# A fused attention and mixture-of-experts kernel: the value product moved ahead of two max products, and side work spread over the slots

## The reference

```
x = x + layernorm(attention(layernorm(x)))
    # attention: own layernorm, qkv product, 16 heads of 16 dims,
    # softmax(q k^T / 4) v over 1024 keys, projection, plus the residual
x = x + layernorm(ffn(layernorm(x)))
    # ffn: silu(x w1) * (x w2), layernorm over 128, product w3;
    # 512 tokens of batch 0 are routed besides to the best of 8 experts
    # and to a weighted mix of the shared and the expert result
```

## Time and profile before

| | |
|---|---|
| times of three runs | 983.48, 983.86 and 985.3 us, median 983.86 us |
| the profiled execution's own time | 983.9 us |
| its span | 982.1 us |
| busy share of the span | PE 90%, VectorE 81%, ScalarE 68%, GpSimd 32% |
| mean granted clock of TensorE | 0.968 of full speed |

### The profile page before, as it was taken

The page is one execution under the profiler, slowest core; times in us unless marked ns, Lnnn a source line. Parts: engine busy times, 40 slices in busy tenths (PEclk is TensorE's granted clock), DMA queues, the critical chain, the costliest instruction groups (busy, mean ns, idle before and its releaser), DMA issues. The chain is left out here.

```text
span 982.1 us, 14337 instructions
## 1 busy us (share of the span) xinstructions
PE 882.3 (90%) x5188; PEld 319.8 (33%) x5188; DVE 792.7 (81%) x1568; ACT 663.7 (68%) x728; POOL 314.5 (32%) x450
## 2 busy tenths in 40 slices
PE   6879999999999999999999999999989989757985
PEld 3312322222243233322332242322322313136863
DVE  4598879898979878899888879889799788265765
ACT  5128778787877787878877868788677768901110
POOL 4041010005424414139443423255243232822113
PEclk9769999999999999999999999999999989988998
DMA  5631010310320203101411022004310001240001
GB/s 143 105 45 39 16 53 16 73 41 10 90 61 13 93 12 70 38 13 55 89 61 56 12 39 59 23 7 105 91 56 14 11 13 31 85 172 23 1 1 64
DMA packets 52375, 49.08 MB, mean 50 GB/s; under 512 B 17504, under 2 KB 43696, under 8 KB 51920
## 3 DMA queue, kind: packets, MB, share of 16 engines
q1 hardware_dynamic: 51680, 46.91, 19.4%
q0 software_dynamic: 384, 1.05, 0.3%
q10 hardware_dynamic: 240, 0.20, 0.2%
HBM read 18.06 MB, written 9.17 MB: 28 GB/s over the span
## 5 line engine op out<-in xcount | busy, mean ns | idle before, releaser
L1331 DVE TENSOR_REDUCE mx<-ring 128x1 f32<-128x512 f32 x1024 | 633.9, 680 | 110.3 <-PE ring L1038 109.6
L873 ACT ACTIVATE prob<-sc,unscale 128x1024 f32<-128x1024 f32 x512 | 539.1, 1113 | 85.2 <-PE sc L1056 83.9
L1038 PE MATMUL ring<-kp,qp 48*128 48x512 f16 x1024 | 299.4, 395 | 43.5 <-DVE mx L1331 22.5
L1070 PE MATMUL obank<-prob,vaug 128*32 128x512 f32 x2048 | 276.1, 612 | 0.7 <-ACT prob L873 0.6
L1038 PEld LDWEIGHTS ring<-kp,qp 48*128 48x128 f16 x1024 | 74.1, 93 | 361.4 <-DVE mx L1331 301.3
L1056 PE MATMUL sc<-qp,kp 64*128 64x512 f16 x1024 | 167.9, 381 | 14.0 <-ACT prob L873 13.3
L644 POOL TENSOR_TENSOR parts<-qkf,parts 128x1024 f16<-128x1024 f32 x14 | 29.9, 2134 | 209.6 <-ACT parts L803 209.6
L1056 PEld LDWEIGHTS sc<-qp,kp 64*128 64x128 f16 x1024 | 50.4, 95 | 92.3 <-ACT prob L873 83.9
L631 POOL TENSOR_TENSOR hid<-hid,b 128x512 f32<-128x512 f32 x24 | 30.2, 1270 | 110.9 <-ACT hid L827 110.9
L639 POOL TENSOR_TENSOR yA<-yA,sums 128x512 f32<-128x512 f32 x15 | 19.0, 1269 | 131.1 <-DMA sums<-reciprocal_scratch 131.1
L1070 PEld LDWEIGHTS obank<-prob,vaug 128*32 128x32 f32 x2048 | 40.5, 108 | 61.5 <-issue 58.4
(11 more groups left out here) (221 smaller groups left out, 749.2 us busy)
## 6 DMA issues: line engine op xcount, KB each, us to landing
x_sb<-x SPq DMA_DIRECT2D x7, 1024.0 KB, 6.0
kp<-parts SPq DMA_DIRECT2D x48, 128.0 KB, 4.4
qp<-parts SPq DMA_DIRECT2D x93, 64.0 KB, 5.5
out<-hid SPq DMA_DIRECT2D x4, 1024.0 KB, 5.3
yA<-oT SPq DMA_DIRECT2D x124, 32.0 KB
sums<-reciprocal_scratch SPq DMA_DIRECT2D x31, 128.0 KB
x_scratch<-x SPq DMA_DIRECT2D x3, 1024.0 KB, 4.5
qp<-mp SPq DMA_DIRECT2D x128, 2.0 KB
```

What stands on the lines that cost most here:

```text
L873: nc.scalar.activation(prob[:, e % 2, 2 * a:2 * a + 2, :].rearrange("p g n -> p (g n)"), sbuf2[a][:, :], ACT.Exp, scale=unscale[:, 0:1]).t ...
L1038: nc.tensor.matmul(dst[:, :], qp[rows, qh, h, qt * P:(qt + 1) * P], kp[rows, h, kh * HALF:(kh + 1) * HALF], start=True, stop=True).then_in ...
L1070: ins = nc.tensor.matmul(obank[i * VW:(i + 1) * VW, :], vaug[:, b % 2, kt, c0:c0 + VW], prob[:, v % 2, i, :], start=(kt == 0), stop=(kt == ...
L1331: nc.vector.tensor_reduce(mx[:, u % 2, n:n + 1], src[:, :], AX.X, ALU.max).then_inc(rv_free, 1)
```

## The change

In `value_product`'s place the PE loop now runs V ahead of M2 and M3 instead of behind them. The tables are written so that (but for mt) no slot holds two items: where two stood in one slot, they stand in neighbouring or next but one slots. `Z_STATS`, `Y_STATS` and a new `U_STATS` put VectorE's statistics beside them, four tiles of 128 tokens at a time or two, the gate runs at tau 50 and 53 (before: 47 and 49), and ScalarE's and GpSimd's steps that feed or follow them move by a few slots.

```
-QK_AT = (2, 2, 4, 4)
-Z_AT = ((18, 18, 20, 20), (9, 9, 17, 17))
-V_AT = (25, 25, 49, 49)
+QK_AT = (1, 2, 4, 5)
+Z_AT = ((17, 19, 21, 23), (9, 11, 13, 15))
+V_AT = (26, 28, 51, 53)
...
+                if 0 <= e - 1 < NS:
+                    value_product(e - 1)
                 if t < NS:
                     max_products(range(2, 4))
-                if 0 <= e - 1 < NS:
-                    value_product(e - 1)
...
-                if 1 <= w < B and tau in (47, 49):
-                    n = int(tau == 49)
+                if 1 <= w < B and tau in (50, 53):
+                    n = int(tau == 53)
...
+                    for i in slots_of(tau, U_STATS):
```

More of the change, by code:

```diff
@@ L44 @@
 QK_LEAD = (4, 5, 6, 7)
-QK_AT = (2, 2, 4, 4)
-Z_AT = ((18, 18, 20, 20), (9, 9, 17, 17))
-V_AT = (25, 25, 49, 49)
[L48 to L53, removed]
+QK_AT = (1, 2, 4, 5)
+Z_AT = ((17, 19, 21, 23), (9, 11, 13, 15))
+V_AT = (26, 28, 51, 53)
+P_AT = (17, 19, 22, 24)
+QK_NEXT_AT = (33, 35, 37, 39)
+X_AT = (41, 42, 43, 44)
+H_AT = (45, 46, 48, 49)
+U_AT = (57, 58)
+W_AT = (59, 60, 61, 62)
 MT_AT = (2, 9, 17, 25, 33, 41, 49, 57)
-Z_STATS = ((9, 10), (2, 2))
-Y_STATS = (21, 21, 25, 25)
+Z_STATS = ((9, 10), (1, 2))
+Y_STATS = (19, 22, 24, 26)
 X_STATS = (33, 35)
-F_AT = ((4, 4), (0, 1))
-D_AT = (43, 51, 14, 19)
+U_STATS = (51, 53)
+F_AT = ((4, 5), (0, 1))
+D_AT = (43, 51, 14, 20)
 ROWS = 16 * (1 + GH)
@@ L692, in _ @@
                         add("p", w - 1, i)
-                if 1 <= w < B and tau == 25:
+                if 1 <= w < B and tau == 27:
                     mean_of("y", w - 1, 0, D)
@@ L699, in _ @@
                     nc.gpsimd.tensor_tensor(x1[:, :, :], x1[:, :, :], x_sb[:, :, :], ALU.add).then_inc(s_x1, 1)
-                if w + 1 < B and tau == 34:
+                if w + 1 < B and tau == 36:
                     second_part(w + 1, 0)
@@ L715, in _ @@
                         add("w", w - 1, i)
-                if 1 <= w < B and tau == 50:
+                if 1 <= w < B and tau == 54:
                     mean_of("u", w - 1, 0, F)
@@ L880, in _ @@
                     nc.scalar.activation(oT[:, u % 2, :], obank[:, :], ACT.Copy).then_inc(s_oT, 1)
-                if 1 <= w < B and tau in (46, 48):
-                    i = int(tau == 48)
+                if 1 <= w < B and tau in (48, 51):
+                    i = int(tau == 51)
                     sc.wait_ge(s_added["h"], 4 * (w - 1) + 2 * i + 2)
@@ L1440, in _ @@
                     nc.vector.tensor_tensor(half, half, sums[0:GH * HD, 1, :], ALU.mult).then_inc(s_div64, 1)
-                if 1 <= w < B and tau in (47, 49):
-                    n = int(tau == 49)
+                if 1 <= w < B and tau in (50, 53):
+                    n = int(tau == 53)
                     gate_first(2 * (w - 1) + n, act[:, 4 * n:4 * n + 4, :], hid[:, 4 * n:4 * n + 4, 0:F])
                     gate_second(2 * (w - 1) + n, act[:, 4 * n:4 * n + 4, :], hid[:, 4 * n:4 * n + 4, F:2 * F])
-                if 1 <= w < B and tau == 49:
-                    ve.wait_ge(s_mean["x"], w)
-                    for i in range(2):
+                if 1 <= w < B:
+                    for i in slots_of(tau, U_STATS):
+                        if i == 0:
+                            ve.wait_ge(s_mean["x"], w)
                         ve.wait_ge(s_hc, 4 * (w - 1) + 2 * i + 2)
                         ins = stats_of("u", act, 4 * i, 4, F)
-                    ins.then_inc(s_stats["u"], 1)
+                        if i == 1:
+                            ins.then_inc(s_stats["u"], 1)
                 for key in RING_AT[t]:
```

## The result

The changed kernel takes 1060.0 us (median of 4 runs, 1059.8 to 1061.6) against 984.5 us for the kernel before on the same chip: 1.077 times as long, interval 1.075 to 1.079. The forecast was 1058.0 us. The profiled execution's span is 1058.1 us at a mean granted clock of 0.971 (before 0.968).

What follows compares the result with a forecast made beforehand. Two loops of equal length, VectorE and M0's bank through V, were taken to bound the slot at 2.49 us. Slots 813.7 plus 8.7, 5.4, 0.9 and 3.6 gave 832.3 against 758.2 us, so 1058.0 us; range 1030 to 1088.

Steps and rivals of the forecast that it cites:

- The slot without an item: V to V with no item: M1 waits for M2's bank, S and V behind it; 2.93 us against 2.49 before.
- Items: Slots holding items or mt: heavy 3.90 us, light 3.55, mt alone 3.55, mt and heavy 4.75, mt and light 4.06.
- The gain of the change: A pair of slots with two heavy items: 7.80 us now against 8.63 before, 0.83 us less a pair.
- ScalarE behind qk items: Bare slots behind 18 qk items: second score waits for late exponentials, 0.3 us each, 5.4 us in all.
- VectorE's other work: Statistics and gate steps ahead of M0's reduction: free where they fit VectorE's idle time, otherwise 8.7 us together.
- The clock: TensorE's clock at the 1.2 GHz level after long waits: two slots, 1.8 us more each, 3.6 us.
- rival 2: Clock falls often because bare slots now have a gap on PE: about 1095 us, 1075 and up; chance 0.13.
- Rival 1: M1's wait for the bank of M2 or M3 costs nothing: faster, about 940 us; chance 0.04.
- GpSimd's steps: GpSimd's chains sit 3 slots or more ahead of who needs them; closest is u; nothing added.
- Head and tail: Parts in front of and behind the slots, without V and M2 both or a moved item PE waits for: unchanged.
- The sum: V of slot 13 to V of slot 255: 832.3 us against 758.2 before, 74.1 us more.

Runs made afterwards that it cites:

- halved maxima: Changed kernel with VectorE reducing only half the keys of one maximum of four, slots 14 to 255: M2's halved 1012.1 us, M0's halved 1056.1 us.

## Why the prediction was right

Point by point, by the steps of the prediction.

- **The slot without an item**: 2.93 us forecast, 2.92 measured; VectorE's idle time 0.44 us forecast and measured; PE's wait for the bank "some 0.9 us" at the weight load, 1.03 measured. The step on which 58 of the 74 us rested is that only M3 and M0 stand between M2 and the M1 that waits for its bank, while S and V both stand between M1 and the next M2. The halved maxima show it.
- **Items**: light 3.55 forecast, 3.52 measured; mt alone 3.55 and 3.52; mt with a light item 4.06 and 4.02. Heavy was set too low, 3.90 against 3.99 to 4.00, because I took half of a pair's 3.65 us for one item, and the 0.1 us that a pair pays once was missed; with mt 4.75 against 4.84 to 4.91, of which 0.1 us has the same reason. Sixty items by some 0.1 us are 6 us too little. The gain of the change, 0.83 us a pair by the forecast, was 0.63 (2 x 4.00 against 8.63).
- **ScalarE behind qk items**: 0.3 us for each of 18 slots forecast; they take 3.08 us, so 0.16 us. 2.5 us too much.
- **VectorE's other work**: 8.7 us forecast. The slots in which it shows, over 2.92 us or over their class: tau 51 1.06 and tau 54 0.61 in two batches each; in batch 3 0.23 (slot 219), 0.67 (226), 0.78 (228), 0.79 (243), 0.25 (244) and 1.69 (246). Together 7.8 us. The gate's price at tau 50 showed one slot later than I wrote, ahead of the v item.
- **The clock**: two slots by 1.8 us forecast. One stretch was at the low level, behind the statistics at tau 53 of batch 3; two slots took 4.65 and 3.95 us, 2.8 us more than 2 x 2.92. The slot at the low level is the 4.7 us of the forecast. (The tail's row counts 72 records, not the 71 of the prediction, which changes nothing.) The windows of PE, columns as in the earlier trace rows:

```profile
870.00:872.00 2.00, 0.77 (x2) 1.00 0.23 53
...
874.00:876.00 2.00, 1.80 (x7) 0.50 0.00 0
...
880.00:882.00 2.00, 1.43 (x14) 1.00 0.00 0
```

  PE was busy for 0.77 of 2 us: M3 and the next M0 waited for banks that VectorE had still to reduce, behind the gate and the statistics. The granted clock then fell to 0.50 and was back at 1.00 within some 8 us. The bare slots, with a gap of 0.57 us each in the records, did not bring it down: over the stretch from 78 to 872 us, which holds 126 of the 131, it was 1.00 (PE busy for 690.8 of 794 us). So rival 2 did not come. The Trainium skill, page "TensorE: Matmul & The Clock Gate", section "A second HAM failure mode: psum-queue depth-cycling", has the clock swing where PE idles briefly while it cycles through PSUM banks; the trace does not agree in these slots.
- **Rival 1**, the bank that never holds PE, would have needed both waits to be absent; both are in the trace.
- **GpSimd's steps** added nothing: the slots with u items, behind the closest of its chains, take 4.02 and 3.52 us, as their classes do.
- **Head and tail** were left alone; they took 2.9 us more (0.7 and 2.2 us), and the cause of most of that is open.

The sum came within 1.0 us of the trace (832.3 against 831.3 us), and that is partly luck, because its errors have both signs: the items 6 us too little, the clock, ScalarE and VectorE terms 4 us too much, and the 0.01 to 0.04 us by which the other classes were set too high another 3. The kernel's time came out 2 us above the forecast (1060.0 against 1058.0) because of head and tail.

## What to carry to other kernels

With a ring of n banks, write down for each product the wait for the bank n places before, and what stands on the in-order engine between the waiting product and the next one that the reader needs. A long product is worth most between a product that fills a bank and the one that waits for it; here the value product covered such a wait and was moved to where it covered none. An item can take over as cover, but only in the slots that have one, and wholly only if its length exceeds the wait (the heavy items here did, the light ones did not): so choose the order by slot and not for all of them. And where a loop is suspected, shorten one link and then, as a control, an equal piece of work outside of it.

## What the runs showed that I had not expected

- A group of f32 items costs about 0.1 us once, ahead of or behind it: one item 1.92 us (109.31 to 111.23), two in a row 3.65 us. Spreading 60 of them is 6 us. What in the engine costs it is not shown.
- Two kernels of equal VectorE load differ by 44 us (1012.1 and 1056.1 us) through the place in the slot at which 0.27 us is spared.
